# Layer norm terms made group by group inside the first and last stage of a three-stage token kernel

## The reference, cut to what matters

```
h = token_pooling(x)                       # 128 x 127 rows of 192: tanh scores, softmax over 4 tokens, projection
h = h + attention(layernorm(h))            # 8 heads, three attentions over thirds of the head, projection
h = h + feed_forward(layernorm(h))         # router picks 1 of 4 experts: gelu(x w1 + b1) w2 + b2, and + x

def layernorm(x, eps=1e-5):                # no weights
    return (x - mean(x)) / sqrt(var(x) + eps)
```

## Time and profile before

| What | Value |
|---|---|
| Time, median of 3 executions (range) | 2083.04 us (2081.87 to 2092.78) |
| Profiled execution: its own time | 2090.13 us |
| Profiled execution: span of its trace | 2088.3 us |
| Mean granted clock of PE over the span | 0.97 of full speed |
| Busy: PE, PEld, DVE, ACT, POOL | 92%, 57%, 71%, 67%, 56% |
| First stage | from 26.3 to 460.1 us |
| First norm stage | 460.4 to 483.3 us |
| Attention stage | 483.6 to 1587.3 us |
| Second norm stage | 1587.6 to 1610.5 us |
| Last stage | 1610.8 us to the end |
| POOL, power of 128 columns (L394) | 2 instructions, 20.79 us each |
| DVE, `bn_stats` (L346, L699) | 128 each, 0.36 and 0.35 us |

### The profile page before, as it was taken

One profiled execution on the slowest core, in us unless ns is written; L12 is line 12 of the kernel. 1 busy time (PEld: TensorE's weight loads), 2 busy tenths in 40 slices (PEclk: granted clock), 3 DMA queues, 4 the chain that ended last, 5 costly groups with the idle time before them and its releaser, 6 DMA issues. The chain is left out here.

```text
span 2088.3 us, 60141 instructions
## 1 busy us (share of the span) xinstructions
PE 1928.8 (92%) x20800; PEld 1200.6 (57%) x20800; DVE 1485.7 (71%) x3636; ACT 1400.0 (67%) x2978; POOL 1166.2 (56%) x2198
## 2 busy tenths in 40 slices
PE   3999999974999999999999999999992799999998
PEld 3999999971444444444444444444441466666666
DVE  4555555544899999999999999999981454554554
ACT  1333333331888888888888888888882566676665
POOL 1111111126677777777777777777755655665661
PEclk9999999995999999999999999999996799999999
DMA  5444444411444444444444444444440333223322
GB/s 143 127 117 118 120 119 117 117 56 37 81 85 89 85 89 89 85 89 89 85 89 87 87 88 87 87 89 87 87 74 10 56 62 71 64 59 70 70 60 54
DMA packets 512121, 176.03 MB, mean 84 GB/s; under 512 B 452168, under 2 KB 511307, under 8 KB 512075
## 3 DMA queue, kind: packets, MB, share of 16 engines
q1 hardware_dynamic: 512075, 175.43, 38.2%
HBM read 53.79 MB, written 12.48 MB: 32 GB/s over the span
## 5 line engine op out<-in xcount | busy, mean ns | idle before, releaser
L691 DVE TENSOR_REDUCE tops<-p_maxa 128x6 f32<-128x762 f32 x512 | 483.2, 944 | 80.6 <-PE p_maxa L534 80.6
L530 PE MATMUL p_s<-qm,kt 32*128 32x256 f16 x3072 | 432.9, 276 | 1.7 <-ACT probs L648 0.6
L605 PE MATMUL p_o<-probs,vn 127*32 127x256 f32 x6144 | 412.7, 386 | 0.2 <-DVE att L719 0.2
L646 ACT ACTIVATE probs<-p_s 128x512 f32<-128x512 f32 x512 | 305.7, 597 | 143.2 <-PE p_s L530 113.3
L693 DVE TENSOR_REDUCE tops<-p_maxb 128x4 f32<-128x508 f32 x512 | 346.1, 676 | 0.0
L530 PEld LDWEIGHTS p_s<-qm,kt 32*128 32x128 f16 x3072 | 162.1, 91 | 271.5 <-issue 126.3
L534 PE MATMUL p_maxa<-kt,qt 24*128 24x256 f16 (+1 forms) x2048 | 294.3, 250 | 21.2 <-DMA kt<-qk 9.3
L651 ACT ACTIVATE probs<-p_s 128x512 f32<-128x512 f32 x512 | 309.9, 605 | 0.0
L648 ACT ACTIVATE probs<-p_s 128x512 f32<-128x512 f32 x512 | 303.3, 592 | 0.0
L965 DVE TENSOR_TENSOR gel_lo<-gel,gel_hi 128x512 f16<-128x512 f32 x192 | 147.0, 766 | 217.1 <-ACT gel_hi L955 215.8
L360 POOL TENSOR_TENSOR diag<-ident,weight 128x256 f32<-128x256 f32 x128 | 78.7, 615 | 368.7 <-DVE band L339 328.5
(11 more groups left out here) (186 smaller groups left out, 4589.8 us busy)
## 6 DMA issues: line engine op xcount, KB each, us to landing
xn<-in_xn SPq DMA_DIRECT2D x32, 768.0 KB, 6.2
xt_a<-in_xt SPq DMA_DIRECT2D x32, 512.0 KB, 4.3
out<-out_sb SPq DMA_DIRECT2D x32, 336.0 KB, 2.7
xt_b<-in_xt SPq DMA_DIRECT2D x32, 256.0 KB, 5.2
xt<-hx SPq DMA_TRANSPOSE x128, 2.3
kt<-qk SPq DMA_TRANSPOSE x128, 2.8
qt<-qk SPq DMA_TRANSPOSE x128, 2.4
qm<-qk SPq DMA_TRANSPOSE x128, 2.7
```

What stands on the lines that cost most here:

```text
L530: return nc.tensor.matmul(o, kt[full(j), r, kind, g, :], qm[full(j), r % 2, versions, g, :], start=True, stop=True, skip_group_check=True)
L605: last = nc.tensor.matmul(p_o[32 * j:32 * j + 32, blocks, :], vn[0:NP, r, src:src + 32], probs[0:NP, r % 2, QUAD * g + j, kind * 256:(kind ...
L646: nc.scalar.activation(probs[:, r % 2, h:h + 2, 512:768], p_s5[:, :, :].rearrange("p (h x) n -> p h (x n)", h=2), ACT.Exp, scale=SCALE).th ...
L691: nc.vector.tensor_reduce(top[:, q, pair, 4:10], p_ma[:, 0:6, 0:NP], AX.X, ALU.max, negate=True).then_inc(dve_ma[u], 1)
```

## The change

The two `norm_terms` stages and the `stats` tensor for all blocks are gone, and attention makes no `bn_stats`. In `tokenize`, body `i` makes the terms of group `i-3` in steps 1 to 3, one per block, with [128 x 4] operands, and POOL one power per group. In `feed_forward` a new `moments` runs `bn_stats` on the four blocks of group `i+4` behind `gel_lo` of chunks 2 to 5, and `sums`, `variance`, POOL's power and `scales` make the terms of group `i+3`; the loop starts two bodies earlier, at -4. ACT's `norm` of a block moves behind the `gel_hi` of its chunk, and the first of a group waits for the scales.

```diff
@@ tokenize, DVE
+            def terms(i, par, step):
+                g = i - 3
+                ...
+                if step == 1:
+                    dve.wait_ge(dve_stats, seen((i - 2) * G))
+                    ...
+                    nc.vector.tensor_tensor(mean[:, :], st[:, :, 1], st[:, :, 4], ALU.add)
+                    nc.vector.tensor_tensor(gap[:, :], st[:, :, 1], st[:, :, 4], ALU.subtract)
+                    nc.vector.tensor_tensor(var[:, :], st[:, :, 2], st[:, :, 5], ALU.add).then_inc(dve_norm, 1)
+                elif step == 2:
+                    dve.wait_ge(dve_norm, seen((i - 2) * 4 - 3))
+                    nc.vector.tensor_tensor(gap[:, :], gap[:, :], gap[:, :], ALU.mult)
+                    nc.vector.tensor_scalar(var[:, :], var[:, :], 1.0 / C, EPS, ALU.mult, ALU.add).then_inc(dve_norm, 1)
+                    dve.wait_ge(dve_norm, seen((i - 2) * 4 - 2))
+                    nc.vector.scalar_tensor_tensor(out=var[:, :], in0=gap[:, :], scalar=0.25, in1=var[:, :],
+                                                   op0=ALU.mult, op1=ALU.add).then_inc(dve_norm, 1)
+                elif step == 3:
+                    dve.wait_ge(pool_root, seen(i - 2))
+                    nc.vector.tensor_copy(t.rstd[:, bass.ds(g * G, G)], root[:, :])
+                    nc.vector.scalar_tensor_tensor(out=t.shift[:, bass.ds(g * G, G)], in0=mean[:, :], scalar=-0.5, ...)
@@ tokenize, DVE body, behind the band of block k and ahead of its bn_stats
+                    terms(i, par, k)
@@ tokenize, POOL body, behind the diagonal of k == 2
+                    if k == 2 and within(i - 3, NG):
+                        pool.wait_ge(dve_norm, seen((i - 2) * 4 - 1))
+                        nc.gpsimd.tensor_tensor(root[:, :], var[:, :], t.half[:, :], ALU.pow).then_inc(pool_root, 1)
@@ attend, DVE
                 maxima(i, r, 0)
-                if within(i - 3, NB):
-                    dve.wait_ge(dve_h, seen(i - 2))
-                    nc.vector.bn_stats(t.stats[:, bass.ds((i - 3) * 6, 6)], t.h[:, bass.ds((i - 3) * C, C)])
@@ feed_forward
-            for i in range(-2, 3):
+            for i in range(-4, 3):
@@ feed_forward, ACT
-            def norm(i, k):
+            def norm(i, r, k):
                 n = (i + 2) * G + k
                 if within(i + 2, NG):
+                    if k == 0:
+                        act.wait_ge(dve_norm, seen((i + 3) * 4))
                     act.wait_ge(pool_x, seen(n - 1))
                     ...
                 for c in range(HCH):
-                    if c < G:
-                        norm(i, c)
                     if within(i, NG):
                         ...
                         nc.scalar.activation(ghi[:, c % 3, :], gel[:, c % 2, :], ACT.Copy).then_inc(act_hi[c], 1)
+                    if c < G:
+                        norm(i, r, c)
@@ feed_forward, DVE
+            def moments(i, r, k):                      # bn_stats of block k of group i + 4
+                ...
+            def sums(i, r):                            # three operations on group i + 3
+                ...
+            def variance(i):                           # three operations, two waits on its own results
+                ...
+            def scales(i, r):                          # rstd and shift
+                if within(i + 3, NG):
+                    dve.wait_ge(pool_root, seen(i + 4))
+                    if within(i + 1, NG):
+                        dve.wait_ge(act_ln, seen((i + 2) * G))
+                    ...
             def body(i, r, half):
                 ...
+                sums(i, r)
                 for c in range(2, HCH):
                     low(i, c)
+                    moments(i, r, c - 2)
+                    if c == 2:
+                        variance(i)
+                scales(i, r)
@@ feed_forward, POOL
             def body(i, r, half):
+                four(i, r)                             # the four blocks, as before
+                if within(i + 3, NG):
+                    pool.wait_ge(dve_norm, seen((i + 4) * 4 - 1))
+                    nc.gpsimd.tensor_tensor(root[:, :], var[:, :], t.half[:, :], ALU.pow).then_inc(pool_root, 1)
@@ audio_tower
-        norm_terms(nc, t, NB, "first_")
         attend(nc, t, NB)
-        norm_terms(nc, t, NB, "second_")
```

More of the change, by code:

```diff
@@ L173, in tokenize @@
         pe_att, act_att, pe_h, act_h = sem("pe_att"), sem("act_att"), sem("pe_h"), sem("act_h")
-        dve_stats = sem("dve_stats")
+        stats = sb("stats", [128, 2, G, 6])
+        mean, gap, var, root = (sb(x, [128, G]) for x in ("mean", "gap", "var", "root"))
+        dve_stats, dve_norm, pool_root = sem("dve_stats"), sem("dve_norm"), sem("pool_root")
         block = ctx.enter_context(nc.Block())
@@ L317, in softmax @@
                         .then_inc(dve_up, 1)
+            def terms(i, par, step):
+                g = i - 3
+                if not within(g, NG):
+                    return
+                st = stats[:, 1 - par]
+                if step == 1:
+                    dve.wait_ge(dve_stats, seen((i - 2) * G))
+                    if not isinstance(i, int) or i > 3:
+                        dve.wait_ge(dve_norm, seen((i - 3) * 4))
+                    nc.vector.tensor_tensor(mean[:, :], st[:, :, 1], st[:, :, 4], ALU.add)
[11 more added lines that the diff above has]
+                    nc.vector.tensor_copy(t.rstd[:, bass.ds(g * G, G)], root[:, :])
+                    nc.vector.scalar_tensor_tensor(out=t.shift[:, bass.ds(g * G, G)], in0=mean[:, :], scalar=-0.5, in1=root[:, :],
+                                                   op0=ALU.mult, op1=ALU.mult).then_inc(dve_norm, 1)
             def body(i, par, half):
@@ L803, in feed_forward @@
         one = sb("f_one", [128, 1])
+        stats = sb("f_stats", [128, 2, G, 6])
+        mean, gap, var, root = (sb("f_" + x, [128, G]) for x in ("mean", "gap", "var", "root"))
+        rstd, shift = sb("f_rstd", [128, 2, G]), sb("f_shift", [128, 2, G])
         p_log = ps("f_log", [128, G, NE])
@@ L929, in _ @@
         def _(act):
[L930 removed]
+            def norm(i, r, k):
                 n = (i + 2) * G + k
                 if within(i + 2, NG):
+                    if k == 0:
+                        act.wait_ge(dve_norm, seen((i + 3) * 4))
                     act.wait_ge(pool_x, seen(n - 1))
                     nc.scalar.activation(hn[:, k % 2, :], t.h[:, bass.ds(n * C, C)], ACT.Identity,
[L935 removed]
+                                         scale=rstd[:, r % 2, k:k + 1], bias=shift[:, r % 2, k:k + 1]).then_inc(act_ln, 1)
             def body(i, r, half):
                 for c in range(HCH):
[L939 to L940 removed]
                     if within(i, NG):
@@ L1019, in body, with four @@
             def body(i, r, half):
+                four(i, r)
+                if within(i + 3, NG):
+                    pool.wait_ge(dve_norm, seen((i + 4) * 4 - 1))
+                    nc.gpsimd.tensor_tensor(root[:, :], var[:, :], t.half[:, :], ALU.pow).then_inc(pool_root, 1)
+            def four(i, r):
                 if not within(i + 2, NG):
@@ L1044, in audio_tower @@
         t.h = sb("h", [128, NB * C])
-        t.stats = sb("stats", [128, NB * 6])
         t.rstd = sb("rstd", [128, NB])
         t.shift = sb("shift", [128, NB])
-        t.half = sb("half", [128, NB])
+        t.half = sb("half", [128, G])
         t.ident = sb("ident", [128, 128])
```

25 lines of the change are left out of this document (23 added, 2 removed).

## The result

The changed kernel takes 2094.82 us (median of 8 runs, 2091.46 to 2097.54), the kernel before 2084.31 us (8 runs, 2081.86 to 2092.78). The ratio is 1.0045, 95% interval 1.0033 to 1.0057: slower by 10.5 us. The forecast was +38 us; direction and range held, the size did not. The profiled execution of after took 2094.31 us, span 2092.5; that of before 2090.13, span 2088.3.

What follows compares the result with a forecast made beforehand. The prediction took the tensor engine as the bound, plus two norm stages where nothing overlaps. Terms -21.2 - 23.7 + 4.3 + 43 + 36 gave +38 us, 2121.4 us on the median's scale, range 2085 to 2143.

Steps and rivals of the forecast that it cites:

- Removed stages: Norm stages before attention and before the last stage: removing them saves 21.2 us and 23.7 us.
- Start of the last stage: DVE's added statistics and terms stand ahead of POOL's first operation there: +4.3 us (3.5 to 6).
- First stage and attention: Added DVE and POOL work hides in the first stage's idle time; attention's removed bn_stats only filled a hole: 0 each.
- rival 3: Attention is bound by DVE: 20 of 34 us come back, 2101 us, or 2066 if the clock holds; chance 0.07.
- The new wait: Last stage, router behind the transpose of f_xt: 1.8 us wait per group, period 15.5 us, +43 us over 30 groups.
- the shift: Last stage: a group's last norm starts 3.18 us later, so POOL's end and the transpose come 2.97 us later.
- 0.33 back from the `out_sb` wait: Last stage: gel_lo of chunk 1 can start earlier, which shortens the tensor engine's out_sb wait by 0.33 us.
- Rival 2: Router behind the transpose: no new wait, period stays 14.07 us, time 2042.4 us; chance 0.13.
- The clock: Last stage: each new router wait brings a half-clock stretch costing 1.2 us per group (0 to 1.7), +36 us.
- nearer to the first: The 1.8 us router wait resembles attention's 1.04 us wait with a half-clock stretch, rather than the last stage's harmless 0.68 us.
- Rival 1: Last stage: clock holds at 1.00 despite the new wait, +3 us, 2086 us (to 2100); chance 0.20.
- Rival 4: Last stage: clock falls for two stretches a group, +1.7 us x 30 more, up to 2170 us; chance 0.04.

Runs made afterwards that it cites:

- experiment 3: Changed kernel with attention running one bn_stats per block again, into a tile nobody reads: 2096.78 us, ratio 1.0059.
- experiment 1: Kernel before, both norm stages kept, with only ACT's norm of a block moved behind the gel_hi of its chunk: 2123.83 us, ratio 1.0187.
- experiment 2: Changed kernel with the norms back ahead of their gel and DVE's scales moved behind gel_lo of chunk 4: 2048.38 us, ratio 0.9829.
- experiment 8: Changed kernel with only the last of a group's four norms back ahead of its gel: 2075.72 us, ratio 0.996.
- experiment 10: Changed kernel with one extra 64-column POOL multiplication, unread, in each group's last block: 2118.85 us, ratio 1.0168.
- experiment 6: Changed kernel with one extra 192-column POOL addition, unread, in each group's last block: 2154.56 us, ratio 1.0364.
- experiment 4: Changed kernel with two extra 192-column POOL additions, unread, in each group's last block: 2166.63 us, ratio 1.0387.
- experiment 9: Changed kernel with norms back ahead of gel, scales behind gel_lo of chunk 4, plus a small DVE memset block before attention: 2043.08 us, ratio 0.9798.
- experiment 7: Kernel before with only the first norm stage removed, its terms made group by group in the first stage: 2068.72 us, ratio 0.9921.

## Why the prediction was right and wrong

**Removed stages: right.** -21.1 and -23.6 against -21.2 and -23.7. The power of 4 columns is 1.01 us, inside 0.65 to 1.2 but above the 0.8 taken; proportion was the worse guide of the two bounds.

**Start of the last stage: right.** POOL is 4.0 us later, of 4.3, and so is the first router: 16.25 us into the stage against 12.18. The second router, from which the balance counts, is 3.05 later, since it stands 9.44 us behind the first and not 10.46.

**First stage and attention: right, and one thing missed.** The cover of the first stage held (+0.55). Attention gained nothing from 31 us less DVE work, as the earlier trace rows said and experiment 3 confirms; rival 3 is out. Missed: a dearer loop jump in attention, +4.1 us, unrelated to any operation of the change. In the pair of profiled executions it is hidden, because that of before had a slow attention of its own: from its start to the start of its last `h` 1102.9 us, where experiment 1, with the same attention code, took 1099.0. The execution of before has two stretches at half clock in its last blocks (0.52 from 1557.40, 0.53 from 1567.60) besides that of the earlier trace rows. That slow attention is one reason why the medians differ by 10.5 us and the traces by 4.2.

**The new wait: right.** The router waits for `f_xt` in every group, and the period is 15.44 us of 15.5. The transpose stands 2.48 us further behind its router than before, where the sum had 2.97 for the shift and 0.33 back from the `out_sb` wait, 2.64 together. Both terms are there, because that wait stands on the loop: `down` of chunk 0 comes ahead of `up` of chunk 3, and the fourth norm behind `gel_hi` of chunk 3. Of the group whose router started at 1809.28 (timelines of the tensor engine and ACT):

```profile
1814.45 0.26 PE L910 MATMUL f_y<-b,f_pkt 128*128 128x192 f16 x1 [0.37 <-DVE out_sb L1005]
...
1818.32 0.53 ACT L938 ACTIVATE f_hn<-h,f_shift,f_rstd 128x192 f32 x1
```

The wait fell from 0.68 to 0.37 us, and the norm starts 9.04 us behind the router, 0.32 less than the 9.36 of the sum (1811.65 less 1802.29). So the 0.33 us came back as forecast. From the norm to POOL it is 0.61 us and not 0.86, and from POOL to the transpose 2.04 and not 1.96; that is the rest. With a slack of 1.1 us (14.07 less 9.21 and 3.75) the period grows by 1.37 us, of 1.45. Experiment 1 shows that the norms' place alone makes it (+38.7 us), experiment 2 that nothing else does. Rival 2, no wait, is out.

**The clock: the step that failed.** The forecast took 1.2 us for each of 30 groups, +36 us. A stretch costs 1.14 us, so the price was right. What failed was its count: 4 of 31 distances. The prediction took it from the earlier trace rows, one wait of 1.04 us in attention with a stretch behind it, and called 1.8 us "nearer to the first". A single event says that a wait can be followed by a stretch, not that it is each time. The same trace has a wait of 0.93 us one block earlier, without a stretch behind it:

```profile
561.19 0.28 PE L534 MATMUL p_maxa<-kt,qt 24*128 24x128 f16 x2 [0.93 <-DMA kt<-qk]
```

And experiment 8 has a wait of 1.0 us in every group, and no stretch. The forecast also reckoned with a wait of 1.8 us. At the wait that came, 1.5 us, the clock mostly holds; at 1.7 us (experiment 10), near the 1.8 reckoned with, over half of the groups are disturbed, 20.9 us. Even there it is not each of the 30 groups, and not the 36 us; the longer waits of experiments 6 and 4 gave 30.6 and 29.4. The Trainium skill (TensorE: Matmul & The Clock Gate, HAM oscillation) describes the mechanism, and its rule of thumb asks for idle gaps longer than any here. At 1.0 and 1.45 us the traces agree with it; at 1.48 us (three to six stretches) and from 1.7 to 3.0 us they don't, and the measurement decides.

**The rivals.** Rival 1, the clock holds, came true: 2086 "to 2100", measured 2094.8, against a chance of 0.20. Without the clock step but with the rest, and 5 us for it, the sum of the prediction is 2121 - 31 = 2090 us; the 4.1 us of the jump make it 2094. Rival 4, two stretches in each group, is out.

## What to carry to other kernels

Where a step is moved behind another in a queue, follow it round the whole loop until the same engine meets it again. The slack is the period less that loop's length, and once it is used up the period is the loop. A wait that shrinks then gives something back only where it stands on that loop, as that for `out_sb` does in the changed kernel and doesn't in experiment 8. Here 2.5 us of later norms cost 41 us, almost all that the two removed stages gave, while the removed stages alone were worth 37 to 43 us (experiments 2 and 9). Before calling work of an engine a saving, look whether it filled a hole. And price a clock stretch by its count over many waits of the same length, not by one.

## What the hardware showed that was not expected

- **Granted clock against the length of a recurring wait.** Between 1.5 and 1.7 us the share of groups with a half-clock stretch goes from 4 of 31 to 17 of 31, and it doesn't grow further at 2.5 and 3.0 us. Below, at 1.0 and 1.45 us, there are none. The runs change the period along with the wait. Why kernels with a wait of 1.48 us had three to six and experiment 1 none at 1.45 stays open.
- **The jump of a loop has two prices.** Attention's tensor queue idles 0.25 or 0.38 us behind the jump, with identical code in the loop; an edit in front of it changes the one into the other (experiments 7 and 9). The Trainium skill (Runtime: NRT & Kernel Launch, Instruction fetch mechanics) says that a taken branch breaks the sequential fetch, and costs a fetch where the target isn't held. An idle time at each jump fits that; whether a fetch is behind it, and what sets its two values, no run here shows.
- **POOL's power.** 20.79 us for 128 columns and 1.01 us for 4 give, as an estimate from these two sizes, 0.16 us per column and 0.37 us fixed. In the last stage of the changed kernel the median is 1.47 us, in those of experiments 2 and 6 it is 1.02 and 1.01.
- **An operation of POOL can be longer where it meets one of DVE in time.** POOL's addition of 192 columns goes from 0.59 to 1.06 us (experiment 8), a subtraction of it by 0.46 us (experiment 6). An instruction added on POOL can so cost its own time plus what it moves into such a meeting.
